# One opening program for load, first norm and linear attention in a two-layer decoder kernel

## The reference, cut to what matters

```
x = x + L0_attn(norm(x))            # linear attention, 16 heads of 8, chunks of 128
x = x + L0_xattn(norm(x), ctx, mask)# softmax attention to ctx_1024, 16 heads of 8
x = x + L0_ffn(norm(x))             # weights rounded to -1, 0, 1; activations to 8 bits
x = x + L1_attn(norm(x))            # four mamba blocks, then a norm with gain and bias
x = x + L1_xattn(ctx, norm(x), m)   # softmax attention, 16 heads of 64
x = x + L1_ffn(norm(x))             # router, top 2 of 8 experts (8 matrices 128 x 128)

norm(x)  = (x - mean(x)) / sqrt(var(x) + 1e-5)          # over the 128 numbers of a token
L0_attn: q = elu(x Wq^T)+1, k = elu(x Wk^T)+1, v = x Wv^T
         out = (q S + mask(q k^T) v) / (q z + rowsum(mask(q k^T))) + 1e-12; out Wo^T
```

## Time and profile before

| | us |
|---|---|
| median of three executions | 1915.6 (1914.8 to 1916.99) |
| the profiled execution, its own time | 1913.99 |
| its span in the trace | 1912.2 |
| start until the first projection of linear attention | 48.6 |
| linear attention, from there to the first product of x0 | 136.9 |
| share of the span with work: PE, DVE, ACT, POOL | 70%, 75%, 58%, 60% |

### The profile page before, as it was taken

The page is one execution under the profiler, slowest core; times in us unless marked ns, Lnnn a source line. Parts: engine busy times, 40 slices in busy tenths (PEclk is TensorE's granted clock), DMA queues, the critical chain, the costliest instruction groups (busy, mean ns, idle before and its releaser), DMA issues. The chain is left out here.

```text
span 1912.2 us, 23467 instructions
## 1 busy us (share of the span) xinstructions
PE 1336.5 (70%) x6930; PEld 664.4 (35%) x6931; DVE 1442.0 (75%) x2464; ACT 1111.3 (58%) x2443; POOL 1141.0 (60%) x742
## 2 busy tenths in 40 slices
PE   3777798985565566656555656565436899999868
PEld 2555465553221122212111211121103566666523
DVE  3554688977329999999999999999992766666634
ACT  2443787875545656665556566655534777777720
POOL 2101465640049999999999999999970443343400
PEclk8899899995676777787777777877668899999978
DMA  3000000000134323242334313323303000000000
GB/s 104 1 2 2 1 2 1 1 1 1 23 155 178 155 117 125 114 178 114 152 155 177 152 69 137 155 114 151 155 0 89 1 1 1 2 1 1 1 0 22
DMA packets 51983, 134.53 MB, mean 70 GB/s; under 512 B 19076, under 2 KB 28568, under 8 KB 39448
## 3 DMA queue, kind: packets, MB, share of 16 engines
q1 hardware_dynamic: 49112, 130.78, 18.2%
q10 hardware_dynamic: 2496, 2.36, 0.4%
q0 software_dynamic: 256, 0.01, 0.0%
HBM read 114.26 MB, written 18.87 MB: 70 GB/s over the span
## 5 line engine op out<-in xcount | busy, mean ns | idle before, releaser
L1498 POOL TENSOR_TENSOR ma_hs<-ma_dtuR,ma_Bt 128x1024 f32<-128x1024 f32 x256 | 596.9, 2359 | 20.4 <-PE ps L1574 12.9
L1657 ACT ACTIVATE ps<-ma_dtR,ma_A 128x512 f32<-128x512 f32 x512 | 332.6, 681 | 345.6 <-DVE ma_hs L1791 286.7
L820 POOL TENSOR_TENSOR x_pr<-x_pr,x_rec 128x512 f32<-128x512 f32 x256 | 267.8, 1046 | 341.6 <-DVE x_rec L1062 341.6
L1785 DVE TENSOR_TENSOR_SCAN ps<-ps,ma_hs 128x1024 f32<-128x1024 f32 x176 | 401.7, 2282 | 0.0
L1574 PE MATMUL ps<-ma_hs,ma_fold 128*32 128x512 f32 x1024 | 179.1, 835 | 206.2 <-POOL ma_hs L1506 174.1
L1028 ACT ACTIVATE x_pr<-x_sm,x_mx 128x256 f32<-128x256 f32 x512 | 255.1, 501 | 52.3 <-DVE x_mx L1053 48.5
L1791 DVE TENSOR_TENSOR ma_hs<-ps,ma_Ct 128x1024 f32<-128x1024 f32 x176 | 215.4, 1224 | 6.1
L1541 PE MATMUL ps<-ma_hn,ma_w_tap 128*128 128x512 f32 (+3 forms) x256 | 144.8, 719 | 96.0 <-ACT ma_hn L1675 84.2
L1785 DVE TENSOR_TENSOR_SCAN ma_hs<-ps,ma_hs 128x1024 f32<-128x1024 f32 x80 | 182.5, 2281 | 34.1 <-ACT ps L1657 32.2
L1506 POOL TENSOR_TENSOR ma_hs<-ma_hs,ma_Ct 128x1024 f32<-128x1024 f32 x80 | 188.4, 2355 | 22.9 <-DVE ma_hs L1785 22.9
L885 PE MATMUL ps<-ident,x_pr 128*128 128x128 f32 x1024 | 160.5, 283 | 5.2 <-DVE x_pT L958 4.6
(11 more groups left out here) (308 smaller groups left out, 2224.6 us busy)
## 6 DMA issues: line engine op xcount, KB each, us to landing
ma_dtuR<-ma_dtu_d SPq DMA_DIRECT2D x32, 1024.0 KB, 6.7
ma_dtR<-ma_dt_d SPq DMA_DIRECT2D x32, 1024.0 KB, 8.6
ma_Bt<-ma_bc_d SPq DMA_DIRECT2D x16, 1024.0 KB, 5.0
ma_Ct<-ma_bc_d SPq DMA_DIRECT2D x16, 1024.0 KB, 6.9
ma_dtu_d<-ma_dtu SPq DMA_DIRECT2D x32, 256.0 KB, 2.0
ma_dt_d<-ma_dt SPq DMA_DIRECT2D x32, 256.0 KB, 2.3
ma_cwb<-in_L_attn_conv_w_dram SPq DMA_DIRECT2D x4, 512.0 KB
x_m<-in_mask_BxSxS_fk_dram SPq DMA_DIRECT2D x1, 2048.0 KB, 11.8
```

What stands on the lines that cost most here:

```text
L820: pool.tensor_tensor(pr[:, r, :, :], pr[:, r, :, :], rec[:, r, :].unsqueeze(2).broadcast_to([P, 2, L]), ALU.mult).then_inc(pr_done, 1)
L1498: pool.tensor_tensor(hs[:, k % SLOTS, :, :], dtuR[:, unit(f, h), q, :].unsqueeze(1).broadcast_to([P, 2, CH]), rows(Bt, k), ALU.mult).then_ ...
L1657: e = act.activation(c.ps[:, 2 * (k % 2) + a, :], dtR[:, unit(f, h), q, :], ACT.Exp, scale=A[:, (f // QUARTERS) % 2, h, q, no:no + 1])
L1785: dve.tensor_tensor_scan(out, pair(k), slot(k), 0.0, ALU.mult, ALU.add).then_inc(scan_done, 1)
```

## The change

The two stages become one, `opening_stage`, without the barrier between them. In it:

- x is loaded first, in two halves with a semaphore each, then ctx, the mask and the feed-forward weights, all on SP's queue. ACT's queue carries only `wa` and `wr`. The expert matrices `we` are loaded much later, in n5, and turned in the expert stage.
- POOL makes the constants of linear attention first and issues its eight small loads after them.
- TensorE turns x, begins the norm, turns `wa` between the two products of the norm, and turns ctx behind the first projection of linear attention (`context_turned`).
- What only later stages need is made on DVE between the pairs of linear attention (`for_later`), 18 operations spread over sequences 0 to 7. One small product goes into sequence 4 (`weight_mean`), the 12 transposes of the rounded weights behind the last sequence (`ternary_turned`).
- In each norm ACT loads one table set by name, `natural_log_exp_and_others`, and then goes Ln, Exp, Ln, Exp by chunks, where before all Ln came ahead of all Exp. This holds in x0, feed-forward, n4, n5, x1 and the expert stage too.

The core of the diff (new line numbers of the changed kernel: norm at L136 to L145 and L194 to L205, opening L222 to L696):

```diff
@@ class Norm, on_scalar (the same in norm_stage)
+        act.preload_act_table_set("natural_log_exp_and_others")
         for h in range(4):
             act.wait_ge(centred, base + h + 1)
             act.activation(self.sq[...], c.ps[:, h, :], ACT.Square).then_inc(squared, 1)
         for h in range(4):
             act.wait_ge(var_done, base + h + 1)
             act.activation(self.lnv[...], c.ps[:, 4 + h, :], ACT.Ln, bias=c.eps[:, 0:1]).then_inc(lnv_done, 1)
-        for h in range(4):
             act.wait_ge(lnv_done, base + h + 1)
             act.activation(self.rstd[...], self.lnv[...], ACT.Exp, scale=-0.5).then_inc(rstd_done, 1)
@@ opening_stage, sync
+                sp.dma_start(xt[:, 0:NT // 2, :], x[:, 0:NT // 2, :]).then_inc(x_in0, 16)
+                sp.dma_start(xt[:, NT // 2:NT, :], x[:, NT // 2:NT, :]).then_inc(x_in1, 16)
+                sp.dma_start(ct[:, :, :], ...).then_inc(ctx_in, 16)
+                sp.dma_start(mi[:, :, :], ...).then_inc(mask_in, 16)
...
@@ opening_stage, tensor
+                for h in range(4):
+                    pe.wait_ge(x_in0 if h < 2 else x_in1, 16)
+                    for k in range(4):
+                        mm = pe.transpose(c.ps[:, 4 + h, k * P:(k + 1) * P], xt[:, 4 * h + k, :], c.ident[:, :])
+                    mm.then_inc(x_turned, 1)
+                for h in range(4):
+                    pe.wait_ge((x_dve, x_act)[h % 2], 1 + h // 2)
+                    pe.matmul(c.ps[:, 4 + h, :], c.centre[:, :], c.xT[:, chunk(h)], ...).then_inc(centred, 1)
+                pe.wait_ge(wa_in, 16 * 9)
+                for n in range(2):
+                    for k in range(4):
+                        mm = pe.transpose(c.ps[:, 2 + n, k * P:(k + 1) * P], wa[:, 4 * n + k, :], c.ident[:, :])
+                    mm.then_inc(wa_turned, 1)
+                for h in range(2):
+                    pe.wait_ge(squared, h + 1)
+                    pe.matmul(c.ps[:, h, :], c.average[:, :], sq[:, chunk(h)], ...).then_inc(var_done, 1)
+                pe.wait_ge(wa_copied, 4)
...
+                pe.wait_ge(normed, 4)
...
                 project(0)
+                context_turned()
                 project_values(0)
...
+                        if b == 4 and m == 0:
+                            weight_mean()
...
                 weigh(B - 1, NG - 1)
+                ternary_turned()
                 out_projection(B - 1)
@@ opening_stage, vector
+                def for_later(b, m):
+                    if (b, m) == (0, 6):
+                        dve.wait_ge(mask_in, 16)
+                        dve.tensor_scalar(c.maskrow[:, :, :], mi[:, :, :], 0.0, MASKED, ...)
+                    if (b, m) == (1, 6):
+                        dve.wait_ge(mask_done, 1)
+                        dve.tensor_reduce(c.present[:, :], c.maskrow[:, :, :], AX.X, ALU.max)
...
                         if m == 7 and b >= 1:
                             finish(b - 1)
+                        for_later(b, m)
                 divide(B - 1)
+                dve.wait_ge(qturned, 1)
+                dve.tensor_copy(c.wguT[:, :], c.psb(2)[:, 0:8 * P])
+                dve.tensor_copy(c.wdT[:, :, :], c.psb(4)[:, 0:4 * P]...)
                 finish(B - 1)
@@ expert_stage, tensor and scalar
+                pe.wait_ge(c.we_in, 16)
+                for e in range(NE):
+                    mm = pe.transpose(c.ps[:, 1 + e // 4, ...], c.we[:, e, :], c.ident[:, :])
...
+                for a in range(2):
+                    act.wait_ge(we_turned, a + 1)
+                    act.activation(ewT[:, 4 * a:4 * a + 4, :]..., c.ps[:, 1 + a, :], ACT.Copy)
@@ decoder_kernel, prefetch in n5
+            sp.dma_start(c.we[:, :, :], g["ew"].rearrange("e h d -> h e d")).then_inc(c.we_in, 16)
```

More of the change, by code:

```diff
@@ L493, in _ @@
             def _(pe):
+                for h in range(4):
[5 more added lines that the diff above has]
+                    pe.wait_ge((x_dve, x_act)[h % 2], 1 + h // 2)
+                    pe.matmul(c.ps[:, 4 + h, :], c.centre[:, :], c.xT[:, chunk(h)], start=True, stop=True).then_inc(centred, 1)
@@ new lines, in _ @@
+                pe.wait_ge(wa_in, 16 * 9)
[5 more added lines that the diff above has]
+                    pe.wait_ge(squared, h + 1)
+                    pe.matmul(c.ps[:, h, :], c.average[:, :], sq[:, chunk(h)], start=True, stop=True).then_inc(var_done, 1)
+                pe.wait_ge(wa_copied, 4)
@@ new lines, in _ @@
+                pe.wait_ge(squared, 3)
+                pe.matmul(c.ps[:, 2, :], c.average[:, :], sq[:, chunk(2)], start=True, stop=True).then_inc(var_done, 1)
+                pe.wait_ge(squared, 4)
+                pe.matmul(c.ps[:, 3, :], c.average[:, :], sq[:, chunk(3)], start=True, stop=True).then_inc(var_done, 1)
+                pe.wait_ge(lnv_done, 1)
+                pe.transpose(c.ps[:, 0, 0:NE], wr[:, :], c.ident[0:NE, 0:NE]).then_inc(wa_turned, 1)
+                pe.wait_ge(normed, 4)
@@ new lines, in context_turned, with weight_mean @@
+                def context_turned():
+                    pe.wait_ge(ctx_in, 16)
+                    for n in range(4):
+                        for k in range(4):
+                            mm = pe.transpose(c.ps[:, 2 + n, k * P:(k + 1) * P], ct[:, 4 * n + k, :], c.ident[:, :])
+                        mm.then_inc(ctx_turned, 1)
+                def weight_mean():
+                    pe.wait_ge(sums, 3)
+                    pe.wait_ge(v_done, 5)
+                    pe.wait_ge(rec_done, 5)
+                    pe.wait_ge(x_done, 3)
+                    pe.matmul(c.ps[:, W, 0:3], c.ones_sq[:, :], part[:, :], start=True, stop=True).then_inc(mean_done, 1)
@@ new lines, in ternary_turned @@
+                def ternary_turned():
+                    pe.wait_ge(ternary, 3)
+                    pe.wait_ge(sc_act, B * NPAIR - 1)
+                    pe.wait_ge(sc_dve, B * NPAIR - 1)
+                    for n in range(8):
+                        pe.transpose(c.psb(2)[:, n * P:(n + 1) * P], wgq[:, n, :], c.identb[:, :])
+                    for n in range(4):
+                        mm = pe.transpose(c.psb(4)[:, n * P:(n + 1) * P], wdq[:, n * P:(n + 1) * P], c.identb[:, :])
+                    mm.then_inc(qturned, 1)
@@ L579, in _ @@
             def _(act):
+                for i, n in enumerate(("aq", "ak", "av", "ao", "xq", "xk", "xv", "xo")):
+                    act.dma_start(wa[:, i, :], g[n]).then_inc(wa_in, 16)
+                act.dma_start(wr[:, :], g["rw"]).then_inc(wa_in, 16)
+                act.preload_act_table_set("natural_log_exp_and_others")
+                for h in (1, 3):
+                    act.wait_ge(x_turned, h + 1)
+                    act.activation(c.xT[:, chunk(h)], c.ps[:, 4 + h, :], ACT.Copy).then_inc(x_act, 1)
+                for h in range(4):
+                    act.wait_ge(centred, h + 1)
+                    act.activation(sq[:, chunk(h)], c.ps[:, 4 + h, :], ACT.Square).then_inc(squared, 1)
+                for h in range(4):
+                    act.wait_ge(var_done, h + 1)
+                    act.activation(lnv[:, chunk(h)], c.ps[:, h, :], ACT.Ln, bias=c.eps[:, 0:1]).then_inc(lnv_done, 1)
+                    act.wait_ge(lnv_done, h + 1)
+                    act.activation(rstd[:, chunk(h)], lnv[:, chunk(h)], ACT.Exp, scale=-0.5).then_inc(rstd_done, 1)
                 def exponentials(b):
@@ L609, in _ @@
                 exponentials(0)
+                act.wait_ge(ctx_turned, 2)
+                act.activation(c.cT[:, chunk(1)], c.ps[:, 3, :], ACT.Copy).then_inc(ctx_act, 1)
                 act.wait_ge(member_done, 1)
```

303 lines of the change are left out of this document (129 added, 174 removed).

## The result

Median 1874.2 us (1873.23 to 1875.61, 4 runs) against 1916.3 in the runs beside it: ratio 0.9778, 95% interval 0.9761 to 0.9795. The forecast was 1883 with 1875 to 1890. The direction was right; the forecast gain was too small. The profiled execution has a span of 1872.6 against 1912.2 before, so 39.6 us went where 32.3 were forecast.

What follows compares the result with a forecast made beforehand. No engine was taken as saturated throughout, each stage having its own limit, the opening a chain. 23.9 + 1.0 - 1.0 - 0.4 - 0.6 + 9.4 = 32.3 us off 1913.99 left 1881.7; with 1.6 for the median, 1883, range 1875 to 1890.

Steps and rivals of the forecast that it cites:

- front: Opening up to linear attention's first projection: that projection starts at 24.7 in place of 48.59, 23.9 us gained.
- start of linear attention: First ten us of linear attention: ctx transposes cost, an earlier higher clock gains; 1.0 us gained, between -1.7 and +2.6.
- insertions: Work put between linear attention's pairs: nearly all hidden in gaps, losing 1.0 (reduction), 0.4 (weights' mean) and 0.6 us (end).
- x0, feed-forward, n4: These three norms: two table loads leave the chain of each, 2.0 to 2.1 us gained three times, 6.2 in all.
- tail: From n5 to the end: 2.4 us gained in n5, 0.4 each in the norms of x1 and expert stage.
- the rival of the cold centring: Opening: centring runs at 1.2 GHz (+3.1 us), or `wa` lands late, giving 1887; chance 12%.
- The compare: Mask's compare between pairs of linear attention: its 1.23 us fits into a gap of 1.28, costing nothing.
- The reduction: Mask's reduction behind pair 6 of sequence 1: 2.29 us against a gap of 1.28, 1.0 lost.
- the end: End of linear attention: 12 transposes fill a wait of 1.47 us, but copies ahead of the last residual lose 0.6.
- the 1875 that the prediction worked out with a drain behind each table load: Six table loads in three norms: by the skill page's drain, 6 x 1.38 = 8.3 us more gained; not adopted.
- TensorE's clock falls better: Rival, expert stage: without the slow products in the first three of 16 steps 5 us are gained, 1878; chance 12%.
- the rule weighed in the prediction: Opening: transposes don't count as busy for TensorE's clock, making the new front 3.1 us later; given little weight.

Runs made afterwards that it cites:

- e1: The changed kernel with its six later norms as they were, no table set named there and four Ln before four Exp: 1880.3 us, ratio 0.9809.
- e4: The changed kernel without the twelve transposes of the rounded weights at the end of linear attention: 1876.7 us, ratio 0.9801.
- e12: The kernel before with twelve unused bf16 transposes of the identity in front of linear attention's last output projection: 1912.9 us, ratio 0.9978.
- e3: The kernel before with only the norms' edit, named table set and alternating Ln and Exp in six later norms: 1903.7 us, ratio 0.9940.
- e13: The changed kernel with n5 alone in the old order, four Ln and then four Exp: 1877.1 us.
- e5: The changed kernel with eight unused TensorE products during the expert stage's ranking: 1872.8 us, ratio 0.9770.
- e7: The changed kernel with three unused TensorE products in the pause of each later norm except n4's: 1864.6 us, ratio 0.9726.
- e15: The changed kernel with two unused DVE copies at n5's end, no order of Ln and Exp changed: 1874.0 us.
- e2: The changed kernel with the table set still named but four Ln before four Exp in the six later norms: 1883.1 us, ratio 0.9788 to 0.9843.

## Why the prediction was wrong

| term | forecast | profile |
|---|---|---|
| front | 23.9 | 24.4 |
| start of linear attention | 1.0 | 1.7 |
| insertions (and clock in linear attention) | -2.0 | -1.6 (-0.5) |
| x0's centring | 0 | 3.1 |
| x0, feed-forward, n4 | 6.2 | 6.3 |
| bodies of x0, feed-forward and mamba | 0 | 0.7 |
| tail | 3.2 | 5.6 |
| sum | 32.3 | 39.6 |

- The front's sum held: x 7.86 for 8.0, first Ln 18.35 for 18.8, 1.24 a pair for 1.3, no wait for `wa`. Inside it the rival of the cold centring came true in part, 4.90 for 3.60. The eight transposes of `wa`, 1.04 for 1.8, and the second half of x, turned by 11.7 and not 12.3, paid for that.
- Insertions: the sum was near, its parts were not. The compare doesn't "fit into 1.28": that gap was read in a later sequence, while behind pair 6 of the first sequence the next causal copy followed at once (two copies in 1.22 at 69.72), so the compare delayed it, ACT's copy and the weighing. The reduction cost 0.65 for 1.0, and the end, charged 0.6, nothing.
- Norms: 2.15 each for 2.0 to 2.1 in x0, feed-forward and n4, 2.43 for 2.4 in n5, 0.51 for 0.4 in the last two. But I credited to their edit alone what the opening's one load gives as well in two of them (e1). The measured time is close to the 1875 that the prediction worked out with a drain behind each table load. That is luck: two loads less made a norm 2.15 shorter, as reckoned without a drain, and the gain came from the clock.
- The step that failed is the clock's term. "TensorE's clock falls better" had 12% and 5 us, in the expert stage only; the forecast itself held the clock of x0's centring and of everything behind it as it was. 3.1 of the 7.3 missed stand in x0's centring. Both numbers were in the earlier trace rows, 3.60 and 6.73, and I had counted twelve transposes into the wait in front of it, as cost only. e4 and e12 show that they bring the lower number. Another 2.4 are the tail, where 3.45 of work taken away returned 5.6. The rival's sign was right there: the steps gave 4.5 of its 5, while x1's centring (5.04 to 6.25) and the way from the expert norm to the steps (26.6 to 27.7) lost 2.3. e1 and e3 tie this to the norms' edit; what makes the clock fall where it does stays open, since in e13 2.43 put back cost 0.1. The remaining 1.8 are small: 0.5 in the front, 0.7 at the start of linear attention, 0.7 in the bodies, and the insertions and norms nearly even.

That transposes keep the clock up speaks once more against the rule weighed in the prediction from the Trainium skill ("TensorE: Matmul & The Clock Gate", Part 4: PE-mode transpose): e12 added nothing but transposes, and 6.73 became 3.67. In the new front the higher clock came later than the rows before had led me to expect, 16 transposes and three slow passes on, which cost 1.3 and not the 3.1 of the rule.

## What to carry to other kernels

Where TensorE waits a microsecond or more ahead of products on the critical path, put later transposes there, or products into a free bank (three a norm gained 9.6 us), and look where the low clock goes instead, since in e5 it moved onto the busiest stage. Name a common ACT table set once, early, and read the loads before you credit later edits. Don't add up small gains behind such stages: 0.51 to 3.45 us of added work cost between 0.1 and 5.5 there, so time each shift. Read a gap at the very place where the work is to go: the gap behind pair 6 was 1.28 in one sequence and none in the first.

## What I had not expected of the hardware

Unused work made kernels faster (e7 9.6, e12 4.1; e15, with 1.2 us added, was level with after). From n5 to the end the span took 473.6 to 473.8 in all four kernels with the old order in n5, x1 and the expert stage (before, e1, e2, e12), with the granted clock of the steps 0.85 or 0.86. It took 468.2 to 468.4 in the eight with that order in one of them or none and nothing added there, with 0.96. There was nothing in between: a norm's order put back alone, worth 0.51 or 2.43, left the sum where it was.
